# Graph attention kernel: one product of the segment maxima for each chunk, 128 weight columns wide, in place of two of 125

## What is computed

```python
e = a_src[src] + a_dst[dst]
e = jax.nn.leaky_relu(e, NEG_SLOPE)
m = jax.ops.segment_max(e, dst, num_segments=N)
e = jnp.exp(e - m[dst])
denom = jax.ops.segment_sum(e, dst, num_segments=N)
alpha = e / denom[dst]
msg = alpha[:, :, None] * h[src]
out = jax.ops.segment_sum(msg, dst, num_segments=N)
```

## Time and profile before

| what | value |
|---|---|
| median of three executions | 5386.51 us |
| the profiled execution | 5389.08 us |
| its span | 5387.1 us |
| TensorE products / weight loads, busy share | 75% / 58% |
| VectorE, ScalarE, GpSimd, busy share | 48%, 29%, 40% |
| V (line 753), products in both layers | 3712 |
| mean granted TensorE clock of the execution | 0.74 |

### The profile page before, as it was taken

The page is one execution under the profiler, slowest core; times in us unless marked ns, Lnnn a source line. Parts: engine busy times, 40 slices in busy tenths (PEclk is TensorE's granted clock), DMA queues, the critical chain, the costliest instruction groups (busy, mean ns, idle before and its releaser), DMA issues. The chain is left out here.

```text
span 5387.1 us, 88957 instructions
## 1 busy us (share of the span) xinstructions
PE 4039.5 (75%) x21808; PEld 3103.1 (58%) x21809; DVE 2565.4 (48%) x8219; ACT 1551.4 (29%) x4325; POOL 2179.4 (40%) x2095
## 2 busy tenths in 40 slices
PE   5177777777777768866377776667766899999999
PEld 3155555555555557744255444445544688888888
DVE  7266666666666775545244344444444542122121
ACT  2122222222222213322122222222222333333333
POOL 0366666666666013246555555555555000000000
PEclk9566666666666559977566666666666899999999
DMA  3233333333335214434333333333335100000000
GB/s 100 69 83 80 82 81 81 81 82 81 80 81 76 80 48 161 159 97 111 76 79 76 77 77 76 77 79 75 76 76 76 53 6 6 6 6 6 5 5 8
DMA packets 382428, 367.94 MB, mean 68 GB/s; under 512 B 249324, under 2 KB 309388, under 8 KB 382242
## 3 DMA queue, kind: packets, MB, share of 16 engines
q0 software_dynamic: 107072, 272.84, 20.3%
q1 hardware_dynamic: 272774, 92.39, 7.1%
q10 hardware_dynamic: 2396, 0.84, 0.1%
HBM read 324.13 MB, written 41.59 MB: 68 GB/s over the span
## 5 line engine op out<-in xcount | busy, mean ns | idle before, releaser
L684 POOL DMA_INDIRECT g_G<-rows,g_pack x1856 | 1928.9, 1039 | 1453.4 <-PE bank L717 725.4
L717 PE MATMUL bank<-g_G,g_MB 128*125 128x260 f32 x1856 | 769.6, 585 | 58.3 <-DVE g_G L939 28.8
L769 PE MATMUL bank<-g_rhs,g_MT 125*128 125x16 bf16 (+1 forms) x5568 | 217.1, 169 | 786.6 <-issue 577.2
L924 DVE SCALAR_TENSOR_TENSOR acc<-acc,g_c,bank 125x65 f32 (+1 forms) x2320 | 622.7, 317 | 332.6 <-PE bank L717 283.5
L717 PE MATMUL bank<-g_G,g_M 128*125 128x257 f32 x1856 | 741.1, 568 | 8.7 <-issue 3.6
L790 ACT ACTIVATE g_mt_d<-bank,unode 125x256 bf16<-125x256 f32 x928 | 384.1, 464 | 1044.9 <-PE bank L702 542.8
L717 PEld LDWEIGHTS bank<-g_G,g_MB 128*125 128x125 f32 x1856 | 520.2, 294 | 272.7 <-issue 143.4
L769 PEld LDWEIGHTS bank<-g_rhs,g_MT 125*128 125x128 bf16 x5568 | 181.7, 101 | 852.0 <-issue 625.6
L717 PEld LDWEIGHTS bank<-g_G,g_M 128*125 128x125 f32 x1856 | 506.6, 287 | 197.0 <-issue 42.0
L1366 DVE SCALAR_TENSOR_TENSOR X<-bank,e_cw,X 125x256 f32 (+1 forms) x400 | 175.2, 479 | 845.0 <-PE bank L1192 845.0
L1262 ACT ACTIVATE e_h<-bank,e_bi_c,e_sc_c 128x250 f32<-128x250 f32 x800 | 403.6, 555 | 559.6 <-PE bank L1183 421.6
(11 more groups left out here) (300 smaller groups left out, 4400.2 us busy)
## 6 DMA issues: line engine op xcount, KB each, us to landing
g_G<-rows,g_pack POOLq DMA_INDIRECT x1856
acc<-in_edge_attr SPq DMA_DIRECT2D x50, 531.2 KB
g_pack<-edge_pack SPq DMA_DIRECT2D x928, 2.0 KB
g_drow<-edge_dst SPq DMA_DIRECT2D x928, 1.0 KB
expert_out<-x_y SPq DMA_DIRECT2D x54, 256.0 KB
g_qe<-edge_q SPq DMA_DIRECT2D x464, 1.0 KB
rows<-acc SPq DMA_DIRECT2D x25, 253.9 KB
rows<-n_T SPq DMA_DIRECT2D x25, 251.0 KB
```

Source lines behind the costliest of these rows:

```text
L684: nc.gpsimd.indirect_dma_start(G[:, r, q, :], None, rows_d[l], bass.IndirectOffsetOnAxis(ap=pack[:, r, q, 0:1], axis=0)).then_inc(S(p + f" ...
L717: mm_ = nc.tensor.matmul(sum_bank(u)[0:TN, 0:HW], left, G[:, rk, q, :], start=(c == 0), stop=(c == C - 1))
L769: mm_ = nc.tensor.matmul(Xe_ps[:, q * KM * H:(q + 1) * KM * H], MT[:, turn(r, 1, q // CP), q % CP, :], rhs[:, q // C, s, :, :], start=(s = ...
L924: ins = nc.vector.scalar_tensor_tensor(at, at, c1[:, rk, u, h:h + 1], sum_bank(u)[0:TN, h * W:(h + 1) * W], ALU.mult, ALU.add)
```

## The change

For each chunk there is one product instead of two. Its moving operand has 3 × H columns: upper part, flag, rest (12 in layer 0, 3 in layer 1). The result's upper part and rest stand beside each other in PSUM, and VectorE adds them one after the other: the first addition now signals `top_hi`, and a second one behind `merge(2, 3)` adds the rest and signals `top`. The weights are 128 columns wide: `hot` reads 3 columns on into the next chunk's matrix (or, after the last chunk, into 3 columns of zeros that a row of `MB` now has at its end), and the product's last 3 rows in PSUM aren't read. `RS` has three parts in place of two times two.

```diff
--- before.py
+++ after.py
@@ -563,7 +563,8 @@
                 wt = sb(p + "wt", [P, RING, Q, H], F32, sc)
                 M = sb(p + "M", [P, MR, CP, TN], F32, sc)
             G = sb(p + "G", [P, RING, Q, HW], F32, sc)
-            MB = sb(p + "MB", [P, RING, Q, TN], F32 if l == 0 else BF16, sc)
+            MB_row = sb(p + "MB", [P, RING, Q * TN + (P - TN)], F32 if l == 0 else BF16, sc)
+            MB = MB_row[:, :, 0:Q * TN].rearrange("p r (q n) -> p r q n", n=TN)
             MT = sb(p + "MT", [TN, MR, CP, P], BF16, sc)
             mt_d = sb(p + "mt_d", [TN, 2, CP, P], BF16, sc)
             dloc = sb(p + "dloc", [P, RING, Q, H], F32, sc)
@@ -573,7 +574,7 @@
             RUN = LT
             SEL = FB
 
-            RS = sb(p + "RS", [P, 2, 2, Q, H], BF16, sc)
+            RS = sb(p + "RS", [P, 3, Q, H], BF16, sc)
             tabf, tabr = (G[0:TN, RING - 1, 2 * k:2 * k + 2, :].rearrange("p q w -> p (q w)")[:, 0:NT * KT * H].rearrange("p (t k h) -> p t k h", t=NT, k=KT)
                           for k in range(2))
             tab = sb(p + "tab", [TN, NT, 3, KT, H], BF16, sc)
@@ -594,7 +595,7 @@
 
             rowT_ps = bank[0][0:QH, 0:2 * P]
             selT_ps = bank[0][:, 2 * P:2 * P + 2 * QH]
-            V_ps = bank[6][:, 0:2 * QH]
+            V_ps = bank[6][:, 0:3 * QH]
             Xe_ps = bank[6][:, 2 * P:2 * P + KM * QH]
 
             def sum_bank(u):
@@ -602,9 +603,11 @@
 
             def hot(r, q):
 
+
+                row = MB_row[:, r, q * TN:q * TN + P]
                 if l == 1:
-                    return MB[:, r, q, :]
-                return MB[:, r, q, :].bitcast(BF16).rearrange("p (n s) -> p n s", s=2)[:, :, 1]
+                    return row
+                return row.bitcast(BF16).rearrange("p (n s) -> p n s", s=2)[:, :, 1]
 
             def run(eng, slot):
 
@@ -749,8 +752,7 @@
                             if late(i, 2):
                                 after(pe, p + "top", i - 1)
                             for q in range(Q):
-                                for s in range(2):
-                                    mm_ = nc.tensor.matmul(V_ps[0:TN, q * 2 * H:(q + 1) * 2 * H], hot(r1, q), RS[:, s, :, q, :], start=(s == 0), stop=(s == 1))
+                                mm_ = nc.tensor.matmul(V_ps[:, q * 3 * H:(q + 1) * 3 * H], hot(r1, q), RS[:, :, q, :], start=True, stop=True)
                             mm_.then_inc(S(p + "V"), 1)
                         spread(2)
                         spread(3)
@@ -836,7 +838,7 @@
                             act.wait_ge(S(p + "selT"), i)
                             if late(i, 2):
                                 after(act, p + "V", i - 1)
-                            nc.scalar.copy(RS[:, 0, :, :, :].rearrange("p k q h -> p (k q h)"), selT_ps).then_inc(S(p + "RS_hi"), 1)
+                            nc.scalar.copy(RS[:, 0:2, :, :].rearrange("p k q h -> p (k q h)"), selT_ps).then_inc(S(p + "RS_hi"), 1)
                         hit(1)
                         if one:
                             if isinstance(i, int) and i == 1:
@@ -869,12 +871,12 @@
                 @block.vector
                 def _(v):
                     nc.vector.memset(NEQ[:, :], 1.0)
-                    nc.vector.memset(RS[:, 1, 1, :, :], 0.0)
+                    nc.vector.memset(MB_row[:, :, Q * TN:], 0.0)
                     nc.vector.memset(SA[:, :, :], 0.0).then_inc(S(p + "SA_set"), 1)
                     nc.vector.memset(SB[:, :, :], -BIG)
                     v.wait_ge(S(p + "SA_set"), 1)
                     nc.vector.memset(SA[:, :, 0:1], -BIG).then_inc(S(p + "SA_set"), 1)
-                    V4 = V_ps[0:TN, :].rearrange("p (q s h) -> p q s h", s=2, h=H)
+                    V4 = V_ps[0:TN, :].rearrange("p (q s h) -> p q s h", s=3, h=H)
                     Xe4 = Xe_ps.rearrange("p (q k h) -> p q k h", k=KM, h=H)
 
                     nc.vector.tensor_copy(tabf[:, :, 0, :], ad[l][:, :].rearrange("p (t h) -> p t h", h=H)).then_inc(S(p + "tab"), 1)
@@ -1006,7 +1008,7 @@
                         scale(1)
                         if one:
                             v.wait_ge(S(p + "RS_hi"), i)
-                            nc.vector.tensor_tensor(RS[:, 1, 0, :, :].rearrange("p q h -> p (q h)"), selT_ps[:, 0:QH], RS[:, 0, 0, :, :].rearrange("p q h -> p (q h)"),
+                            nc.vector.tensor_tensor(RS[:, 2, :, :].rearrange("p q h -> p (q h)"), selT_ps[:, 0:QH], RS[:, 0, :, :].rearrange("p q h -> p (q h)"),
                                                     ALU.subtract).then_inc(S(p + "RS"), 1)
                         merge(2, 0)
                         scale(2)
@@ -1028,8 +1030,12 @@
                         if one:
                             v.wait_ge(S(p + "gone"), i)
                             nc.vector.tensor_tensor(units(SB)[:, :, 1:K3, :], gone[:, :, :].rearrange("p (u c) h -> p u c h", u=U),
-                                                    V4[:, :, 0, :].rearrange("p (u c) h -> p u c h", u=U), ALU.add).then_inc(S(p + "top"), 1)
+                                                    V4[:, :, 0, :].rearrange("p (u c) h -> p u c h", u=U), ALU.add).then_inc(S(p + "top_hi"), 1)
                         merge(2, 3)
+                        if one:
+                            v.wait_ge(S(p + "top_hi"), i)
+                            nc.vector.tensor_tensor(units(SB)[:, :, 1:K3, :], units(SB)[:, :, 1:K3, :],
+                                                    V4[:, :, 2, :].rearrange("p (u c) h -> p u c h", u=U), ALU.add).then_inc(S(p + "top"), 1)
                         if one:
                             v.wait_ge(S(p + "top"), i)
                             v.wait_ge(S(p + "SA"), i)
```

## The result

The changed kernel took 5345.27 us (median of 5, 5326.19 to 5355.84) against 5387.41 us (5375.51 to 5400.59) for the kernel before: a ratio of 0.9918, with a 95% interval of 0.9891 to 0.9945. It is faster by 42 us, 0.8%, and the forecast was 235 us. The profiled execution has a span of 5324.4 us.

The account below looks back on a forecast made before the run. The prediction took each attention slot as a loop through V, the sums, VectorE's chain and Xe, with GpSimd's gathers limiting layer 1. Layer 0's 147 us plus layer 1's 88 made 235, so 5386.5 - 235 = 5151 us, range 5040 to 5300.

Parts of the forecast that it names:

- What is late next: Attention slots after V shrinks: layer 0 gains 2.5 us a slot, layer 1 only GpSimd's wait, 1.55 us.
- 14.9 us: Layer 1: the gather freed by unit 6's sums stays this far behind unit 2's, so only the wait is gained.
- 58 × 2.5: Layer 0's total: 58 slots times 2.5 us saved each, given as 147 us.
- The 74% of slow blocks: Layer 0: share of V's blocks taken to run at the lower clock, weighting savings of 3.06 and 1.53 us.
- whole saving: Range's fast end, 5040: both layers keep all of V's saving, addition free, 58 × 2.9 + 57 × 2.7 = 322 us.
- 0.46 us: V's block a slot: 16 products with 128 weight columns at line 769's 29 ns each.
- The strict reading: V's weight loads: read 32 bits at a time, a 4-byte stride or mid-word start would gain nothing, as in the first rival.
- The addition: VectorE's second addition ahead of the scan: costs 0.3 us a slot in layer 0, about 0.2 in layer 1.
- The loads don't get faster: Rival for V: only the number of products halves, 136 us saved, 5250 us; chance 0.23.
- the clock takes it back: Rival: sums of units 2 to 5 stay at the lower clock, losing up to 1.8 us a slot, 5360 us; chance 0.07.
- The gathers set the slot: Slower rival: V's saved time becomes waiting and the addition adds 0.3 us a slot, 5421 us; chance 0.06.
- Layer 1 gains more: Rival: 16 fewer products ease Xe's pieces in layer 1, with 6 us a slot below 4950 us; chance 0.04.

Follow-up runs that it names:

- e18: The kernel before with only the first chunk of each unit gathered (half the gathers), with stalls: 4783.90 us.
- e19: The changed kernel with only the first chunk of each unit gathered (half the gathers), with stalls: 4558.33 us.
- e6: The changed kernel with 125 weight columns in V instead of 128, without stalls: 4748.48 us, 0.987 of the kernel before.
- e3: The changed kernel without VectorE's second addition, so the rest of the maxima is left out, without stalls: 0.9821 of the kernel before.
- e2: The kernel before with V's 32 products a slot issued twice, without stalls: 5161.79 us, 1.073 of the kernel before.
- e20: The changed kernel with TensorE's sums of units 6 and 7 moved to just ahead of Xe, with stalls: 5694.83 us, 1.0564 of the kernel before.

## Why the prediction was wrong

**The failed step** is "What is late next": that layer 0's slot would become 24.4 us, "above the 22.3 of the gathers", and that in layer 1 "a slot can gain only the wait, about 1.8 us". For layer 0, 2.36 to 2.5 us were forecast and 0.01 came, for layer 1 1.55 and 0.65. Both steps let what V gives up pass on to the slot. The overlap was wrong, and the runs with stalls show what stood in its place. In layer 0 V is a link of the loop in the forecast; the link from V to VectorE's chain didn't hold: the sums of units 2 to 5 ended 3.6 us earlier after V's start, and the chain for `rhs` 0.2 us earlier (13.86 and 13.66 us). In layer 1 the forecast took GpSimd's wait of 2.10 us for unit 2's sum being late. In the trace of before that sum had ended (by the modelled ends) when GpSimd's stream ran dry in 42 of 52 slots of layer 1 (20 of 52 in layer 0), and GpSimd waited all the same. After the change it had ended in all 104. The mean wait there fell by 1.18 us, in the forecast's direction, but the distance to unit 6's gather didn't stay at "14.9 us": it grew from 14.96 to 15.52 us in the mean, as waits came before units 3 and 4 instead. Where such a wait of over 1.5 us stands in the changed kernel's layer 1 (27 slots), its median is 2.06 us, against 1.92 before, so its size isn't V's doing.

What takes the time away is tied to the stream of gathers, as the pair e18 and e19 shows: with half of it the same change is worth 226 us under the same condition. Why a finished sum is acted on late there is open.

Without stalls the step fails in the plain way for layer 1, whose slot fell by 0.43 us, since before it was within that of its gathers (20.5). Layer 0's slot fell by 1.74 us and met its gathers (22.4). But with half the gathers it fell by 1.92 us, so this cap took only 0.2 us of the 2.5; another 0.6 was missing without it too, where V's block fell by 2.1 us and 2.66 were forecast. My reading of 27 us as one loop through V missed that part of those 27 us was waiting that V's length doesn't change.

**Sums and shares.** 58 × 2.5 is 145 and not 147, so the sum is 233 us and the time 5154. The 74% of slow blocks in layer 0, taken from a mean duration, were 34 of 58, or 59%: V's block was 2.92 us in the mean and fell by 2.32 us, not by 2.66. The "whole saving" of 2.9 us a slot in the range is likewise more than the 2.66 that the forecast's own shares give.

**The right steps.** V at "0.46 us" measured 0.60, in both layers: the stride of 4 bytes and the starts in mid-word do no harm. The Trainium skill, "TensorE: Matmul & The Clock Gate", section on weight-path perf modes, has 128 weights and a type other than FP32 as the condition, and this trace agrees: 104 ns for a load. The strict reading of its description as 32-bit reads, by which these weights would have gained nothing, did not hold. e6 splits the two parts of the change where nothing stalls: fewer products 1.3%, the width a further 0.8%, all of it in layer 0. V's price over both layers, put at 175 to 320 us for halved gathers, came out at 269 and 226 where the gathers were halved. That is in part luck: the term behind it was too high for V, and the gain of the sums behind V, at the higher clock, was not in it.

**The addition** takes 258 ns and 166 ns, as forecast, but 0.3 us of path was too much where it was tested: e3 shows no gain from leaving it out where the gathers set the slot. With half of them it is inside the 1.92 us.

**The rivals.** "The loads don't get faster" is refuted by V's rows, "the clock takes it back" by the sums of units 2 to 5, which run at 0.86 and 0.94 of the full clock where it was 0.65 and 0.68: on balance the clock gave time. "The gathers set the slot" came nearest, but its sign was wrong, as the addition costs nothing there. "Layer 1 gains more" had the right row (Xe's pieces without releaser), and the wrong cause: with 16 products fewer a slot Xe still comes in 5.6 runs (6.3 before) and lasts 5.9 us (7.5 before). I gave the rows that had "issue" as their releaser 4% when 625.6 us of the earlier trace rows's largest idle time, 852.0, were theirs.

**What stays open** is what makes the condition. It comes and goes between groups, slows TensorE and SyncE while gathers stream (SyncE's issues stand up to 1.4 or 2.1 us apart in place of 0.5), and half the gathers take nearly all of it away. The transfers themselves are not slower: a gather's packets take 165 ns in the mean in layer 0 and 163 to 164 in layer 1, with stalls and without, which speaks against slower transfers as the cause. Loading of instructions doesn't go with it either: the trace of the kernel before has 5 packets of instructions in layer 1's slots with stalls and 5 without, and Xe is in most pieces there. That signals are held up and not only recorded late follows from GpSimd and VectorE, which act on them late (the ends of matmuls are modelled, but 16 sums that start at 3112.89 are 3.74 us long in both conditions); which path they share with the gathers, no run shows. The 125 columns, the doubled V and the missing addition (e6, e2, e3) ran only without stalls, so their prices with stalls are not shown. Of the versions tried none beats the changed kernel in both conditions: the early sums are equal without stalls and 350 us slower with them.

## What to carry to other kernels

Idle time ahead of a step says that it is late, not what would make it early. Look, over many slots, at when the step it is said to wait for had ended: if that was before the wait began (42 of 52 slots here), making that step earlier gains nothing by itself. One slot isn't enough: the slot shown above still waits 1.88 us before unit 2's gathers, the mean had fallen to 0.69. Where an engine's own stream, here 16 gathers with their issue, fills three quarters of a loop or more (74% to 98% in the kernel before), work it out for each stage and cap the gain of every other edit by it. Idle time without a releaser belongs in the forecast as a bound of its own, and moving more work into it can lengthen it, as e20 shows.

## What was not expected of the hardware

The same kernel took 4814 and 5389 us in different groups, each within 1%. In the slower condition TensorE ran about 40 of layer 1's 48 Xe products at 29 to 31 ns and most of the rest 0.7 to 1.4 us apart until the gathers paused, and in the slot shown a completion reached VectorE 1.2 us after a gather's end. Shortening V from 2.0 us or more to 0.6 let the sums behind it run at a mean granted clock of 0.94 in place of 0.68 (layer 1). Weight loads of overlapping, odd-aligned or strided bf16 columns ran at 104 ns like contiguous ones.
